# A quantiser's search whose squares are summed 64 wide on VectorE, with GpSimd making chunk products

## The chip, the cores and the metric

The kernel runs on one core of a Trainium2 chip. A core has five engines with a queue of instructions each: TensorE (PE, with its weight loads as PEld) for matrix products, VectorE (DVE), ScalarE (ACT), GpSimd (POOL) and SyncE (SP), which here only starts transfers. The queues run side by side and meet only in semaphores. The metric is the time of one execution on the device, in microseconds, as the median of several.

## The reference

Two transformer-like blocks over x of 4 x 256 x 256. Block 0 is a cross attention and a feed-forward layer whose weights are quantised in the kernel; block 1 is a smooth-quantised gated layer and a layer of product-key experts. The change lies in the quantisation of block 0's feed-forward weights:

```
def mse_quant_dequant(w):                    # w: 1024x256 and 256x1024, in blocks of 64
    wb = w.reshape(O, I // 64, 64)
    amax = jnp.max(jnp.abs(wb), axis=-1, keepdims=True)
    base = jnp.maximum(amax, 1e-08) / QMAX
    ...
    for s in SHRINKS:                        # 16 values, 0.4 to 1.0
        scale = base * jnp.asarray(s, dtype=w.dtype)
        deq = jnp.clip(jnp.round(wb / scale), -QMAX, QMAX) * scale
        err = jnp.sum((deq - wb) ** 2, axis=-1, keepdims=True)
        ...                                  # keep the scale with the least error
    deq = jnp.clip(jnp.round(wb / best_scale), -QMAX, QMAX) * best_scale
...
x = x + _L0_xattn_ref(_layernorm(x, axis=-1), ctx_1024, ...)
x = x + _L0_ffn_ref(_layernorm(x, axis=-1), L0_ffn_w_fc, L0_ffn_w_proj)   # relu(x w_fc^T)^2 w_proj^T
x = x + _L1_xattn_ref(_layernorm(x, axis=-1), fside_BxS2xS2_0, ctx_1024)
x = x + _L1_ffn_ref(_layernorm(x, axis=-1), L1_ffn_Wq, L1_ffn_keys, L1_ffn_e_down, L1_ffn_e_up)
```

## The kernel before

Every engine's program is written out by hand as one queue, and all data sit in one large SBUF tile, `arena`, cut into named pieces. The search for the best scale is the first long stage. The two weight matrices lie as 128 partitions x 4096 columns, four **chunks** of 1024 columns with 16 blocks of 64 in each. A **unit** g (0 to 63) is one chunk with one of the 16 shrink factors.

For each chunk c, VectorE takes the block maxima (`prepare`, L1308 to L1312) and scales the weights (`scale_weights`, L1317); ScalarE takes absolute values (`absolute`, L994) and an upper part (`upper`, L999); GpSimd subtracts to get the lower part (`split`, L332). For each unit:

- ScalarE (odd units, L1005) or VectorE (even units, L1347) clips and rounds the scaled weights into one of eight FP8 buffers (`clip_round`). From unit 8 on it waits until TensorE is done with unit g-6.
- TensorE adds to a pair of PSUM banks (two pairs, by turns) the difference of rounded and exact weights: L553 for a chunk's first two units, later L548, which takes the last but one unit's integers away again, then L560, which adds the new ones.
- ScalarE squares the pair (L1020, L1023) into one of **three** square buffers `qd`.
- GpSimd **folds**: it adds columns 32 to 63 of each block to columns 0 to 31 (L343), into one of four buffers `qf`.
- VectorE sums the 32 columns of each block (`sum_error`, L1352).

After a chunk VectorE chooses the scale (`choose`, L1323 to L1329) and quantises and dequantises the chunk in place (L1334, L1335, L1340). Then TensorE transposes it (`w_transposed`; L431 for chunks 0 and 1, L519 for 2 and 3) and ScalarE copies it out (`weights_out`). Attention, layer norms, the transposes of `e_down` and FFN-1 (`ffn1`, L531, 16 blocks, each followed by a relu, L989, on ScalarE and a square on GpSimd, `square_hidden`, L326) are woven in at fixed units by conditions on g in each engine's loop. FFN-2 (`ffn2`, L592), GUW transposes and everything later come after. The loads of WQ1 and EU are issued when all 64 sums are made.

## Time and profile before

| what | us |
|---|---|
| median of three runs (415.94 to 416.29) | 416.27 |
| the profiled execution | 414.8 |
| its span, first to last instruction | 413.0 |
| PE busy in the span | 346.8 |
| DVE busy | 341.7 |
| ACT busy | 248.3 |
| POOL busy | 170.5 |

Busy times are of the span, and engines run side by side, so they don't add up. Matrix products are pipelined and their ends are modelled. An operation's duration overlaps a little with its neighbour's on the same engine, so sums of durations by group are slightly more than busy time by window.

### The profile page before, as it was taken

Reading aid. Unit: us, or ns where it says so; the run is one execution under the profiler, and the core shown is the slowest. Engines: PE = TensorE matmul, PEld = TensorE weight load, DVE = VectorE, ACT = ScalarE, POOL = GpSimd, SP = SyncE. Lnnn points to the kernel's source line nnn. Section 1 sums busy time; section 2 is a strip of 40 time slices with the busy share of each in tenths; the row PEclk is TensorE's granted clock in tenths of the full one; section 3 lists DMA queues with packets and bytes.
Section 4 is the critical chain, followed back from the end, with each engine's and each line's share of the span. In section 5 each row is a group of like instructions: output and inputs, shape, how many; then the busy total and the mean of one; then the engine's idle time right before and its main releaser. Section 6 shows DMA issues by size and latency. Waiting matters only on the chain.

```text
span 413.0 us, 8385 instructions
## 1 busy us (share of the span) xinstructions
PE 346.8 (84%) x3222; PEld 253.1 (61%) x3222; DVE 341.7 (83%) x877; ACT 248.3 (60%) x371; POOL 170.5 (41%) x203
## 2 busy tenths in 40 slices
PE   2876697738857867979997888999999999989996
PEld 1442474413322323656796776887888888778885
DVE  4999879993898597645878899999989999999950
ACT  4799969967778798312645778864676565211000
POOL 3364654456886989812200110526214127621000
PEclk9999999987997999989999999999899999999999
DMA  8920000000000000350000000000000000000000
GB/s 257 362 79 2 2 0 0 2 1 0 2 0 1 0 2 0 97 160 1 2 0 2 1 2 0 3 2 2 2 5 12 14 2 17 2 14 2 17 14 27
DMA packets 11144, 11.42 MB, mean 28 GB/s; under 512 B 608, under 2 KB 10592, under 8 KB 11104
## 3 DMA queue, kind: packets, MB, share of 16 engines
q1 hardware_dynamic: 11104, 10.88, 8.3%
q8 instruction: 26, 0.43, 0.4%
q14 instruction: 14, 0.11, 0.1%
HBM read 9.83 MB, written 1.05 MB: 26 GB/s over the span
## 4 chain that ended last, share of the span: by engine, by line
DVE 43%; PE 26%; POOL 12%; issue 11%; ACT 6%; DMA 1%; POOLq 0%; DVEq 0%; ACTq 0%
POOL arena L343 10%; PE pair L754 9%; PE pair L592 4%; PE pair L718 3%; DVE i L1554 3%; DVE arena L1614 2%; DVE stats L1274 2%; DVE arena L1352 2%; DVE arena L1610 2%; PE pair L740 2%; DVE s L1548 2%; POOL arena L326 2%; DVE XN L1287 2%; PE pair L531 2%; DVE arena L1317 1%
## 5 line engine op out<-in xcount | busy, mean ns | idle before, releaser
L343 POOL TENSOR_TENSOR arena<-arena 128x512 f32<-128x512 f32 x64 | 89.0, 1403 | 59.0 <-ACT arena L1023 23.3
L718 PE MATMUL pair<-arena,EDT 128*128 128x256 f32 x256 | 60.2, 383 | 0.0
L754 PE MATMUL pair<-EU,arena 128*128 128x256 f32 x256 | 58.4, 382 | 0.6 <-DVE arena L1638 0.6
L1352 DVE TENSOR_REDUCE arena<-arena 128x16 f32<-128x512 f32 x64 | 42.8, 680 | 18.4 <-POOL arena L343 18.3
L548 PE MATMUL pair<-arena,WQ 128*128 128x512 fp8e4 x112 | 35.1, 397 | 22.1 <-ACT arena L1020 18.9
L754 PEld LDWEIGHTS pair<-EU,arena 128*128 128x128 f32 x256 | 47.9, 190 | 7.4 <-issue 1.0
L718 PEld LDWEIGHTS pair<-arena,EDT 128*128 128x128 f32 x256 | 47.1, 190 | 6.5 <-ACT arena L1153 0.2
L393 POOL TENSOR_TENSOR arena<-arena 128x512 f32<-128x512 f32 x20 | 27.1, 1370 | 49.4 <-ACT arena L1145 49.4
L1023 ACT ACTIVATE arena<-pair 128x1024 f32<-128x1024 f32 x32 | 33.3, 1041 | 14.7 <-PE pair L560 14.7
L560 PE MATMUL pair<-arena 128*128 128x512 fp8e4 x128 | 40.5, 399 | 0.0
L1020 ACT ACTIVATE arena<-pair,sq_bias 128x1024 f32<-128x1024 f32 x32 | 36.2, 1131 | 4.6 <-PE pair L560 3.7
L1005 ACT ACTIVATE arena<-arena,clip_bias 128x1024 fp8e4<-128x1024 f32 x32 | 37.2, 1166 | 0.0
L531 PE MATMUL pair<-arena 128*128 128x512 f32 x64 | 34.7, 678 | 1.7 <-ACT arena L980 1.7
L548 PEld LDWEIGHTS pair<-arena,WQ 128*128 128x128 bf16 x112 | 9.9, 101 | 42.4 <-issue 38.8
L1347 DVE TENSOR_SCALAR arena<-arena 128x1024 fp8e4<-128x1024 f32 x32 | 29.7, 930 | 7.0 <-PE pair L560 5.6
L1153 ACT ACTIVATE arena<-pair 128x512 f32<-128x512 f32 x32 | 19.0, 598 | 26.8 <-PE pair L718 26.7
L326 POOL TENSOR_TENSOR arena<-arena 128x512 f32<-128x512 f32 x16 | 20.1, 1260 | 26.0 <-ACT arena L989 26.0
L592 PEld LDWEIGHTS pair<-arena 128*128 128x128 f32 x256 | 29.7, 193 | 1.5 <-issue 1.5
L592 PE MATMUL pair<-arena 128*128 128x128 f32 x256 | 30.2, 276 | 0.0
L1145 ACT COPY arena<-pair 128x512 f32<-128x512 f32 x20 | 19.5, 1070 | 11.1 <-PE pair L740 11.1
L740 PEld LDWEIGHTS pair<-arena 64*128 64x128 bf16 x1536 | 20.1, 93 | 6.2 <-issue 3.2
L370 POOL CAST i12f<-i 128x64 bf16<-128x64 uint32 x8 | 8.0, 1004 | 36.6 <-DVE i L1554 28.9
(196 smaller groups left out, 667.5 us busy)
## 6 DMA issues: line engine op xcount, KB each, us to landing
arena<-in_L_ffn_e_down_dram SPq DMA_DIRECT2D x1, 2048.0 KB, 12.2
EU<-in_L_ffn_e_up_dram SPq DMA_DIRECT2D x1, 2048.0 KB, 9.2
arena<-in_L_ffn_w_fc_dram SPq DMA_DIRECT2D x2, 512.0 KB, 5.3
X<-in_x_dram SPq DMA_DIRECT2D x1, 1024.0 KB, 5.9
arena<-in_L_ffn_w_proj_dram SPq DMA_DIRECT2D x1, 1024.0 KB, 14.6
GUW<-in_fside_BxS2xS_dram SPq DMA_DIRECT2D x1, 1024.0 KB, 12.1
out_dram<-arena SPq DMA_DIRECT2D x8, 128.0 KB, 1.7
CTX<-in_ctx_dram SPq DMA_DIRECT2D x1, 512.0 KB, 4.9
```

The source lines that it names most:

```text
L343: pool.tensor_tensor(qf(g), sq[:, :, 0:32], sq[:, :, 32:64], ALU.add).then_inc(s["folded"], 1)
L531: last = pe.matmul(bank[2 + i % 2], W1T[:, k, m * P:m * P + P], xnT[:, k, half * 512:half * 512 + 512], start=(k == 0), stop=(k == 1))
L548: pe.matmul(to[half], stepN[:, j - 2, :], qr[:, (g - 2) % QDEEP, cols[half]], start=False, stop=False, skip_group_check=True)
L560: last = pe.matmul(to[half], stepI[:, j, :], qr[:, g % QDEEP, cols[half]], start=False, stop=True, skip_group_check=kept)
L592: last = pe.matmul(bk2(F2_BANK[b])[:, n, o * P:o * P + P], h2T[:, k, at:at + P], W2T[:, k, o * P:o * P + P], start=(k == 0), stop=(k == HI ...
L718: last = pe.matmul(bk2(4 + i % 2)[:, r, :], EDT[:, k, at:at + P], xT4[:, b % 2, k, :], start=(k == 0), stop=(k == 1))
L754: last = pe.matmul(bk2(7)[:, n, :], PR[:, n, e, :], EU[:, e, :], start=(e == 0), stop=(e == EROWS - 1))
L1005: act.activation(qr[:, g % QDEEP, :], qu[:, g // NS % 2, :], ACT.Relu, bias=clip_bias[:, 0:1], scale=-GRID / STEPS[g % NS], saturate=False ...
L1020: act.activation(qd[g % 3], pair[2 + g % 2][:, :], ACT.Square, bias=sq_bias[:, g % NS:g % NS + 1]).then_inc(s["squared"], 1)
L1023: act.activation(qd[g % 3], pair[2 + g % 2][:, :], ACT.Square).then_inc(s["squared"], 1)
L1347: dve.tensor_scalar(qr[:, g % QDEEP, :], qu[:, g // NS % 2, :], TB_MAX * STEPS[g % NS], GRID / STEPS[g % NS], ALU.min, ALU.mult, saturate= ...
L1352: dve.tensor_reduce(err[:, g // NS % 2, :, g % NS], qf(g), AX.X, ALU.add).then_inc(s["reduced"], 1)
```

## The change

Nothing is folded any more (`halved` is false for every unit). VectorE's `sum_error` reduces the squares themselves, 128 x 1024, 64 columns a block. There are five square buffers (`QDEPTH`), the two new ones in two places by turns of time. GpSimd takes over, for chunks 1 to 3, `scale_weights`, and for chunks 0 to 2 the product ahead of the rounding (`scale_quantised`) and `dequantise`; it keeps `split` and `square_hidden`. VectorE makes the first `split`. The step tables are made in eight portions with a semaphore each. The loops over g are replaced by lists of calls on each engine, in another order. The arithmetic of each result is otherwise the same.

```diff
+    QDEPTH = 5
-        qd = (cut(22 * KI, CH), cut(23 * KI, CH), cut(7 * KI, CH))
+        qd_early, qd_late = ((cut(22 * KI, CH), cut(23 * KI, CH), cut(7 * KI, CH), cut(a * KI, CH), cut((a + 1) * KI, CH))
+                             for a in (14, 24))
...
+        def halved(g):
+
+            return g < 0
...
+        def qd(g):
+            return (qd_early if g <= QF_LATE else qd_late)[g % QDEPTH]
...
# GpSimd
-            for g in range(NU):
+            def fold(g):
...
-                if g % NS == 12 and g // NS + 1 < NCH:
-                    split(g // NS + 1)
-                if g - 2 in FFN1_UNIT:
-                    square_hidden(FFN1_UNIT[g - 2])
+            def scale_weights(c):
+
+                pool.wait_ge(s["prepared"], c + 1)
+                if c >= 2:
+                    pool.wait_ge(s["diff"], NS * (c - 1))
+                pool.tensor_tensor(blocks(qu[:, c % 2, :]), blocks(W[:, c * CH:c * CH + CH]), spread(rbase), ALU.mult
+                                   ).then_inc(s["scaled"], 1)
+
+            def scale_quantised(c):
+
+                pool.wait_ge(s["chosen"], c + 1)
+                pool.tensor_tensor(blocks(qt), blocks(W[:, c * CH:c * CH + CH]), spread(rscale), ALU.mult
+                                   ).then_inc(s["qscaled"], 1)
+
+            def dequantise(c):
+
+                pool.wait_ge(s["qrounded"], c + 1)
+                pool.tensor_tensor(blocks(W[:, c * CH:c * CH + CH]), blocks(qi), spread(scale), ALU.mult
+                                   ).then_inc(s["wquant"], 1)
...
# ScalarE
+            def square(g):
+
+                act.wait_ge(s["diff"], g + 1)
+                if g >= QDEPTH:
+                    if halved(g - QDEPTH):
+                        act.wait_ge(s["folded"], folds(g - QDEPTH))
+                    else:
+                        act.wait_ge(s["reduced"], g - QDEPTH + 1)
...
# VectorE
             def sum_error(g):
-                dve.wait_ge(s["folded"], g + 1)
-                dve.tensor_reduce(err[:, g // NS % 2, :, g % NS], qf(g), AX.X, ALU.add
-                                  ).then_inc(s["reduced"], 1)
+                if halved(g):
+                    dve.wait_ge(s["folded"], folds(g))
+                    squares = qf(g)
+                else:
+                    dve.wait_ge(s["squared"], g + 1)
+                    squares = blocks(qd(g))
+                dve.tensor_reduce(err[:, g // NS % 2, :, g % NS], squares, AX.X, ALU.add).then_inc(s["reduced"], 1)
...
+            sum_error(47)
+            clip_round(56)
+            sum_error(48)
...
+            sum_error(59)
+            round_quantised(2)
+            sum_error(60)
+            sum_error(61)
+            sum_error(62)
+            sum_error(63)
+            choose(3)
+            scale_quantised(3)
+            round_quantised(3)
+            dequantise(3)
```

Three places show how the order moves. First GpSimd, from the end of its constants to FFN-1's last squares; before:

```order
L343 TENSOR_TENSOR arena<-arena 128x512 x13
L332 TENSOR_TENSOR QP<-arena,QP 128x1024
L343 TENSOR_TENSOR arena<-arena 128x512 x16
L332 TENSOR_TENSOR QP<-arena,QP 128x1024
L343 TENSOR_TENSOR arena<-arena 128x512 x3
L326 TENSOR_TENSOR arena<-arena 128x512
L343 TENSOR_TENSOR arena<-arena 128x512 x4
L326 TENSOR_TENSOR arena<-arena 128x512
```

And after the change, where L372 scales weights, L353 splits, L378 scales for the rounding, L384 dequantises and L347 squares hidden blocks:

```order
L372 TENSOR_TENSOR arena<-arena 128x1024
L353 TENSOR_TENSOR QP<-arena,QP 128x1024
L378 TENSOR_TENSOR arena<-arena 128x1024
L372 TENSOR_TENSOR arena<-arena 128x1024
L353 TENSOR_TENSOR QP<-arena,QP 128x1024
L384 TENSOR_TENSOR arena<-arena 128x1024
L347 TENSOR_TENSOR arena<-arena 128x512 x2
L378 TENSOR_TENSOR arena<-arena 128x1024
L347 TENSOR_TENSOR arena<-arena 128x512
L372 TENSOR_TENSOR arena<-arena 128x1024
L384 TENSOR_TENSOR arena<-arena 128x1024
L353 TENSOR_TENSOR QP<-arena,QP 128x1024
```

The folds are gone, and products of 1024 columns stand between splits and squares. Second VectorE, near the sums of units 16 and 17, where chunk 0's scale is chosen; before (L1352 sums, L1347 clips, L1285 and L1287 a norm):

```order
L1328 TENSOR_TENSOR arena<-arena 128x16
L1329 RECIPROCAL arena<-arena 128x16
L1347 TENSOR_SCALAR arena<-arena 128x1024
L1352 TENSOR_REDUCE arena<-arena 128x16
L1334 TENSOR_TENSOR arena<-arena 128x1024
L1335 TENSOR_SCALAR arena<-arena 128x1024
L1352 TENSOR_REDUCE arena<-arena 128x16
L1285 RECIPROCAL rstd<-rstd 128x2
L1287 TENSOR_SCALAR XN<-X,mv,rstd 128x256 x2
```

And after (L1627 sums, L1617 clips, L1564 to L1570 chunk 2's block maxima, L1603 the rounding):

```order
L1589 TENSOR_TENSOR arena<-arena 128x16
L1590 RECIPROCAL arena<-arena 128x16
L1627 TENSOR_REDUCE arena<-arena 128x16
L1564 TENSOR_REDUCE arena<-arena 128x16
L1565 TENSOR_SCALAR arena<-arena 128x16
L1569 RECIPROCAL arena<-arena 128x16
L1570 TENSOR_SCALAR arena<-arena 128x16
L1617 TENSOR_SCALAR arena<-arena 128x1024
L1627 TENSOR_REDUCE arena<-arena 128x16 x2
L1617 TENSOR_SCALAR arena<-arena 128x1024
```

The product L1334 has left VectorE's queue, and the rounding stands 15 rows behind the reciprocal instead of 4. Third TensorE at the end of the search; before (L519 transposes chunk 3, chunk 2's having stood after unit 58; L592 is FFN-2, x16 one half of a batch):

```order
L548 MATMUL pair<-arena,WQ 128x512 x2
L560 MATMUL pair<-arena 128x512 x2
L531 MATMUL pair<-arena 128x512 x6
L431 MATMUL pair<-ident,GUW 128x128 x4
L592 MATMUL pair<-arena 128x128 x16
L519 MATMUL pair<-ident,arena 128x128 x8
L531 MATMUL pair<-arena 128x512 x2
L592 MATMUL pair<-arena 128x128 x16
```

And after (L608 and L620 are the last unit, L578 transposes, first of chunk 2 and then of chunk 3, L590 is FFN-1, L736 FFN-2):

```order
L608 MATMUL pair<-arena,WQ 128x512 x2
L620 MATMUL pair<-arena 128x512 x2
L578 MATMUL pair<-ident,arena 128x128 x8
L590 MATMUL pair<-arena 128x512 x6
L490 MATMUL pair<-ident,GUW 128x128 x4
L736 MATMUL pair<-arena 128x128 x16
L578 MATMUL pair<-ident,arena 128x128 x8
L590 MATMUL pair<-arena 128x512 x2
```

Chunk 2's transposes now stand between the last unit and the three FFN-1 blocks.

## Rows read from the trace of the kernel before

**Rows 1.** The page: the chain that ended last, share of the span by line.

```profile
POOL arena L343 10%; PE pair L754 9%; PE pair L592 4%; PE pair L718 3%; DVE i L1554 3%; DVE arena L1614 2%; DVE stats L1274 2%; DVE arena L1352 2%; DVE arena L1610 2%; PE pair L740 2%; DVE s L1548 2%; POOL arena L326 2%; DVE XN L1287 2%; PE pair L531 2%; DVE arena L1317 1%
```

**Rows 2.** Windows: length; busy us of PE, PEld, DVE, ACT, POOL; clock, DMA.

```profile
13.10:64.40 51.30, 41.17 (x177) 24.75 (x177) 46.03 (x109) 43.41 (x63) 26.88 (x19) 0.97 0.21 71
64.40:106.40 42.00, 29.23 (x132) 14.81 (x131) 32.99 (x52) 34.51 (x46) 24.84 (x19) 0.92 0.00 1
106.40:171.30 64.90, 49.02 (x172) 20.30 (x171) 52.18 (x67) 51.67 (x58) 56.03 (x40) 0.95 0.00 1
13.10:171.30 158.20, 119.42 (x478) 59.85 (x478) 131.20 (x225) 129.59 (x165) 107.75 (x76) 0.95 0.07 23
...
178.30:413.00 234.70, 218.96 (x2696) 186.14 (x2696) 196.62 (x621) 111.19 (x196) 56.91 (x75) 0.99 0.03 9
```

**Rows 3.** Waits, 13 to 171.3 us: who waited for whom, us, times, longest.

```profile
POOL arena L343 <- ACT arena L1023: 23.3, 11, 10.7
POOL arena L343 <- ACT arena L1020: 22.4, 14, 3.7
...
DVE arena L1352 <- POOL arena L343: 18.3, 19, 1.7
...
POOL arena L343 <- DVE arena L1352: 11.1, 7, 2.0
...
DVE arena L1347 <- PE pair L560: 5.6, 2, 3.9
```

**Rows 4.** Groups on DVE, 0 to 178 us: busy us, mean ns, idle before.

```profile
L1352 DVE TENSOR_REDUCE arena<-arena 128x16 f32<-128x512 f32 x64 | 42.8, 680 | 18.4 <-POOL arena L343 18.3
L1347 DVE TENSOR_SCALAR arena<-arena 128x1024 fp8e4<-128x1024 f32 x32 | 29.7, 930 | 7.0 <-PE pair L560 5.6 <-ACT arena L994 1.2
L1287 DVE TENSOR_SCALAR XN<-X,mv,rstd 128x256 f32<-128x256 f32 x16 | 9.4, 641 | 0.2
L1317 DVE TENSOR_TENSOR arena<-arena 128x1024 f32<-128x1024 f32 x4 | 7.8, 1960 | 0.0
L1334 DVE TENSOR_TENSOR arena<-arena 128x1024 f32<-128x1024 f32 x4 | 6.2, 1547 | 0.0
...
L1340 DVE TENSOR_TENSOR arena<-arena 128x1024 f32<-128x1024 fp8e4 x4 | 5.3, 1336 | 0.0
L1308 DVE TENSOR_REDUCE arena<-arena 128x16 f32<-128x1024 f32 x4 | 4.8, 1209 | 4.3 <-DMA arena<-in_L_ffn_w_fc_dram 4.3
```

**Rows 5.** Groups on POOL, 0 to 178 us.

```profile
L343 POOL TENSOR_TENSOR arena<-arena 128x512 f32<-128x512 f32 x64 | 89.0, 1403 | 59.0 <-ACT arena L1023 23.3 <-ACT arena L1020 22.4 <-DVE arena L1352 11.1
...
L332 POOL TENSOR_TENSOR QP<-arena,QP 128x1024 fp32r<-128x1024 f32 x3 | 7.0, 2349 | 0.0
```

**Rows 6.** Lines by themselves: ns shortest/median/longest, first and last start.

```profile
L1352 DVE TENSOR_REDUCE arena<-arena x64: 655/676/689, 20.0 to 170.6; 128x16 f32<-128x512 f32 x64
...
L1347 DVE TENSOR_SCALAR arena<-arena x32: 662/693/2224, 8.7 to 158.9; 128x1024 fp8e4<-128x1024 f32 x32
...
L1287 DVE TENSOR_SCALAR XN<-X,mv,rstd x32: 400/409/1459, 20.8 to 337.7; 128x256 f32<-128x256 f32 x32
...
L1324 DVE TENSOR_TENSOR arena<-arena x4: 425/746/1460, 64.8 to 171.7; 128x256 f32<-128x256 f32 x4
...
L326 POOL TENSOR_TENSOR arena<-arena x16: 1030/1038/2025, 103.1 to 203.9; 128x512 f32<-128x512 f32 x16
```

**Rows 7.** Timeline: start us, length us, engine, what.

```profile
16.52 1.88 PE L458 MATMUL pair<-ctxT,arena 128*128 128x512 f32 x4
```

**Rows 8.** Timeline at the end of the search.

```profile
166.08 5.31 PE L531 MATMUL pair<-arena 128*128 128x512 f32 x12
...
171.66 3.74 PE L592 MATMUL pair<-arena 128*128 128x128 f32 x32
...
174.97 1.22 DVE L1334 TENSOR_TENSOR arena<-arena 128x1024 f32<-128x1024 f32 x1
...
178.23 1.09 PE L519 MATMUL pair<-ident,arena 128*128 128x128 f32 x8 [2.83 <-DVE arena L1340]
```

More of the change, by code:

```diff
@@ L257, in on_act, with act_rounds @@
         def on_act(g):
-            return 0 < g < NU and g % 2 == 1
+            return g % 2 == 1
+        def act_rounds(g):
+            return sum(on_act(i) for i in range(g + 1))
         @block.sync
@@ L349, in _ @@
+            dequantise(2)
+            square_hidden(7)
             square_hidden(8)
@@ new lines, in _ @@
+            unit(7)
+            probs_transposed(0)
+            x_transposed(1)
+            unit(8)
+            unit(9)
+            x_transposed(2)
+            probs_transposed(1)
+            unit(10)
+            attend(0)
+            probs_transposed(2)
+            unit(11)
+            attend(1)
+            attend(2)
+            unit(12)
+            x_transposed(3)
+            unit(13)
+            unit(14)
+            probs_transposed(3)
+            unit(15)
+            unit(16)
@@ new lines, in _ @@
+            unit(25)
+            unit(26)
+            unit(27)
+            unit(28)
+            x1_transposed(1)
+            unit(29)
+            unit(30)
+            unit(31)
+            unit(32)
+            x1_transposed(2)
+            unit(33)
+            unit(34)
+            w_transposed(0)
+            unit(35)
+            unit(36)
+            x1_transposed(3)
+            unit(37)
+            ffn1(0)
+            unit(38)
+            ffn1(1)
+            ffn1(2)
+            unit(39)
@@ new lines, in _ @@
+            unit(40)
+            ffn1(3)
+            unit(41)
+            unit(42)
+            unit(43)
+            unit(44)
+            unit(45)
+            w_transposed(1)
+            unit(46)
+            unit(47)
+            unit(48)
+            unit(49)
+            unit(50)
+            ffn1(4)
+            unit(51)
+            unit(52)
+            unit(53)
+            unit(54)
+            ffn1(5)
+            unit(55)
+            unit(56)
+            ffn1(6)
+            unit(57)
@@ L587, in ffn2 @@
+            ffn1(7)
+            unit(58)
+            unit(59)
+            unit(60)
+            unit(61)
+            unit(62)
+            unit(63)
+            w_transposed(2)
             def ffn2(b, o, tiles=range(TPB)):
@@ new lines, in _ @@
+            square(8)
+            probs_out(0)
+            absolute(1)
+            probs_out(1)
+            clip_round(11)
+            x_out(2)
+            square(9)
+            square(10)
+            probs_out(2)
+            clip_round(13)
+            clip_round(15)
+            square(11)
+            exponentials(3)
+            square(12)
+            x_out(3)
+            upper(1)
+            square(13)
+            square(14)
+            probs_out(3)
+            square(15)
+            std(0, 2, "ln2")
@@ new lines, in _ @@
+            x1_out(0)
+            clip_round(25)
+            square(23)
+            clip_round(27)
+            e_down_out(5)
+            clip_round(29)
+            square(24)
+            clip_round(31)
+            square(25)
+            absolute(2)
+            upper(2)
+            square(26)
+            square(27)
+            e_down_out(6)
+            square(28)
+            x1_out(1)
+            square(29)
+            square(30)
+            e_down_out(7)
+            square(31)
@@ new lines, in _ @@
+            clip_round(33)
+            square(32)
+            x1_out(2)
+            clip_round(35)
+            square(33)
+            clip_round(37)
+            square(34)
+            square(35)
+            weights_out(0)
+            x1_out(3)
+            square(36)
+            clip_round(39)
+            relu(0)
+            clip_round(41)
+            square(37)
+            relu(1)
+            square(38)
+            relu(2)
+            square(39)
+            clip_round(43)
+            square(40)
@@ new lines, in _ @@
+            clip_round(45)
+            clip_round(47)
+            square(41)
+            square(42)
+            absolute(3)
+            square(43)
+            upper(3)
+            square(44)
+            relu(3)
+            square(45)
+            clip_round(49)
+            square(46)
+            square(47)
+            clip_round(51)
+            square(48)
+            weights_out(1)
+            square(49)
+            clip_round(53)
+            square(50)
+            square(51)
@@ new lines, in _ @@
+            square(52)
+            relu(4)
+            clip_round(55)
+            square(53)
+            square(54)
+            clip_round(57)
+            relu(5)
+            square(55)
+            clip_round(59)
+            square(56)
+            relu(6)
+            square(57)
+            clip_round(61)
+            square(58)
+            clip_round(63)
+            square(59)
+            relu(7)
+            square(60)
+            square(61)
+            square(62)
+            square(63)
@@ L1054, in c_root @@
+            weights_out(2)
             def c_root(b):
```

458 lines of the change are left out of this document (311 added, 147 removed).

## Prediction

> **What bounds the kernel now.** I read the stages first, then the waits, then the groups of instructions, then the chain at the end of the search.
>
> The stages [rows 2] cut the span at 13.1 us (first difference on TensorE done), at 64.4, 106.4 and 171.3 us (last sum of chunks 0 and 1, and of the whole search) and at 178.3 us (last chunk dequantised). The reader is to see that in the search no engine is full: VectorE is busy 131.2 of 158.2 us, ScalarE 129.6, and TensorE 119.4 by modelled ends. After 178.3 us it is another kernel, TensorE busy 219.0 of 234.7 us. So the search counts until 171.3 us, then the seven microseconds in which VectorE makes the last weights, and then TensorE. The chain that ended last [rows 1] names the culprit: the GpSimd fold, L343, first of all lines with a tenth of the span.
>
> The waits of the search [rows 3] show a ring. GpSimd waits 23.3 and 22.4 us for the squares, VectorE 18.3 us for the folds, and GpSimd 11.1 us for sums that free a folded buffer. Every unit passes TensorE, ScalarE, GpSimd and VectorE, with three square buffers between the second and third; VectorE's 27.0 us of idle time (158.2 - 131.2) is the length of this ring, not work. A change that only moved work between engines would gain little; one that shortens the ring can gain up to these 27 us, less what it adds to VectorE.
>
> **The change, part by part.**
>
> *The fold goes, the sum doubles.* A fold took 1.403 us on GpSimd, 64 times [rows 5]; it and its handover leave the ring. A sum over 128x512 took 0.680 us; over 128x1024 there is a row of the same operation and shape of input, L1308, the block maximum, 1.209 us [rows 4]. Difference 0.529 us, times 64: **+33.9 us** on VectorE. The short sums did not stretch beside a busy GpSimd (655 to 689 ns, [rows 6]), so I take this as it is; with those two for the short sum the bounds are +33 and +35.5.
>
> *Chunk products move to GpSimd.* VectorE loses the scaling of chunks 1 to 3 (four took 7.8 us, the first, the fastest, 1.2 of it: 6.6), the first product of the quantiser for chunks 0 to 2 (6.2 less the last, 1.2 [rows 8]: 5.0) and the dequantisation of chunks 0 to 2 (5.3 - 1.2: 4.1) [rows 4]: **-15.7 us**. On GpSimd these nine have no row. From below a fold's 1.4 us for half the elements; from above twice that, 2.8. The nearest row is the 1024-wide subtraction L332, 2.349 us [rows 5], and I take it. Nine are 21 us on an engine that loses 89 us.
>
> *VectorE's short operations stretch less.* Clips on VectorE (L1347) ran between 662 and 2224 ns [rows 6], mean 930 [rows 4]; 32 at 0.66 would be 21.1 us instead of 29.7, so 8.6 us is stretch. The norms (L1287, 16 at 641 [rows 4] against a fastest of 400 [rows 6]) add 3.9, and the 256-wide operations of the choice and of the attention's normalising, which stretch like L1324 (425 to 1460 ns, [rows 6]), about 3.5 by my estimate: 16 us of stretch in all. I put it down to GpSimd running beside them, since the sums, next to the same GpSimd, don't stretch. GpSimd was busy 107.8 us in the search [rows 2]. In the new search it has 12 operations of 2.35 us and eight squares of hidden blocks at about 1.04 (L326, [rows 6]): 36.5 us, a third. So up to two thirds of the stretch, 10.6 us, go. I take **-10 us**; bounds 0 and -12.
>
> The Trainium skill (SBUF — State Buffer, Who interferes with whom) says that VectorE's `tensor_scalar` in its two-port mode, and its operations with two SBUF inputs, contend with GpSimd for one port pair held for a whole instruction, and that `tensor_reduce` on this chip never does. By that rule all of the stretch is GpSimd's, the relief the whole 10.6 us and the time 406.6 us; if the stretch had another cause, the relief would be 0 and the time 417.2. This trace agrees on the reductions (655 to 689 ns).
>
> VectorE's work from 13.1 us to its last sum is then 131.2 + 33.9 - 15.7 - 10 = 139.4 us: with no idle time the last sum would end at 152.5 us instead of 171.3. ScalarE's list is the same instructions in another order, 129.6 us [rows 2]: second, at 142.7 us.
>
> *Idle time that stays.* Five square buffers instead of three, and the order has VectorE summing two to five units behind ScalarE, so a sum seldom waits. But both engines now have over 85% of the stage to do, in fixed queues, each releasing the other, and in the first 16 units attention is woven in: there VectorE already was busy 46.0 of 51.3 us [rows 2] and now gets 16 longer sums (+8.5 us) and loses one product (2.0) and some stretch. This part gains next to nothing; the gain must come after 64.4 us, where VectorE was busy 33.0 of 42.0 and 52.2 of 64.9 us. I estimate 8 us of idle (between 3 and 16), some 5% of the stage. So the last sum ends near 13.1 + 139.4 + 8 = 160.5 us: **-10.8 us**.
>
> *The start.* TensorE now does the first attention input, 1.9 us at 16.5 us before [rows 7], ahead of unit 0, and VectorE makes step tables in eight portions. I cost this at nothing: up to 20 us VectorE has statistics, tables, clips and the second block maximum to do. Without that cover it costs the 1.9 us.
>
> *The end.* Before, the last unit was followed on TensorE by three FFN-1 blocks (from 166.08 us, 5.3 us), the first gate-weight transpose and half an FFN-2 group (3.74 us from 171.66 us), finished by 175.4 us; it then waited 2.83 us for the last dequantised chunk and began its transposes at 178.23 us [rows 8]. Now the transposes of chunk 2 stand in front of this run, after unit 63, and they need that chunk dequantised by GpSimd. VectorE rounds it four sums, 4.8 us, ahead of the end; with 2.35 us of GpSimd, 1.1 of transposes (as L519, [rows 8]) and the rest of the copies on ScalarE, 0.6 by my estimate, the three FFN-1 blocks start about 0.7 us before the last sum ends instead of 5.2 us before. Their run of 9.4 us (166.08 to 175.4) ends 8.7 us after it, where the last chunk's transposes could begin 7.0 us after it (178.23 - 171.25). **+1.7 us**, bounds 0 and +4. From there TensorE is nearly full and the order is kept, so later stages shift as a block. The two loads that wait for the last sum (WQ1 and EU) also move as a block.
>
> Sum: -10.8 + 1.7 = -9.1 us. The profiled execution took 414.8 us (span 413.0); the median of the three runs shown is 1.5 us more. 414.8 - 9.1 = 405.7, so a median of **407.2 us**.
>
> **Rivals.**
>
> *A, the queues fit almost without gaps.* For it: five buffers, and clips and sums interleaved unit by unit. Against it: ScalarE alone would keep the search going to 142.7 us. Idle time 3 instead of 8 us: 402.2 us.
>
> *B, the two full engines stop each other more.* Idle 13 instead of 8 us, mostly in the attention units: 412.2 us. For it: VectorE was idle only 5.3 us there before, with lighter sums, and now each stall pushes back sums that hold square buffers.
>
> *C, slower: clips wait at the head of VectorE's queue.* The clip of unit g waits for TensorE to be done with unit g-6, and sums stand behind it (clip 56 stands behind sum 47 and needs unit 50). Before, this happened twice, 5.6 us together [rows 3], 2.8 each. Each such wait stops the engine that is now the bound. One is within my 8 us. The gain is gone when more than three others appear (9.1 / 2.8); with four the time is 418.4 us. Against it: VectorE runs behind TensorE when it is the bound, and then the unit is long done.
>
> *D, slower: GpSimd's longer instructions hold VectorE.* A clip that took 2.22 us instead of 0.66 shows a block of about one fold. If half of each of GpSimd's 36.5 us blocked a VectorE operation, stretch would be 18 us, more than now, where the forecast keeps 6: 419.2 us. It turns slower from 15 us of stretch on. Read strictly, the Trainium skill (SBUF — State Buffer, Who interferes with whom) would have it so, as the later engine there waits for the whole instruction; against that, in this trace 107.8 us of GpSimd came with 16 us of stretch, a seventh.
>
> **How the numbers follow.** My forecast 62%, A 12%, B 11%, C 9%, D 6%. A, the forecast and nearly all of B are faster by over 0.2% (0.8 us, about what a measurement of this kernel can tell); B's end and the light ends of C and D give 5% for within 0.2%, and their rest 11% for slower. The range reaches from the middle of A to past B: 402 to 415 us; it leaves out the fast half of A and most of C and D, and holds the bounds of stretch (-12 gives 405.2; 0 gives 417.2, outside, and counts with D) and of the end (405.5 to 409.5).
>
> **What the new profile would show.** 64 sums near 1.2 us each; the VectorE clips' mean down from 930 ns to below 800; VectorE busy 93% or more from 13 us to the last sum, that sum ending near 160.5 us; chunk 0's sums done at 63 to 66 us as before; GpSimd products near 2.35 us and its share of the span from 41% to about 25%; TensorE starting the last chunk's transposes about 9 us after the last sum. I am wrong if long sums take more than 1.25 us, if clips wait for TensorE more than twice, or if VectorE is idle over 16 us in the search.

## The result, and the profile after

The changed kernel takes 389.81 us (median of 4 runs, 389.28 to 390.5), the kernel before, timed beside it, 416.11 us (4 runs, 414.91 to 416.29): a ratio of 0.9375, 95% interval 0.9351 to 0.9398. The gain is 26 us where 9 were forecast: 389.8 us lies below the range of 402 to 415.

First the windows of the changed kernel, to be laid beside [rows 2]: from the first difference to the last sum of the search, the part before chunk 0's choice (it begins at 64.4 us in both kernels), from the last sum to the last chunk's first transpose, and from there to the end.

```profile
13.10:147.20 134.10, 111.76 (x465) 55.55 (x464) 131.84 (x224) 127.81 (x163) 33.53 (x20) 0.96 0.08 28
13.10:64.40 51.30, 46.28 (x221) 27.91 (x220) 49.87 (x120) 50.03 (x74) 4.37 (x2) 1.00 0.21 71
147.20:155.80 8.60, 8.60 (x48) 5.92 (x47) 8.29 (x10) 1.79 (x3) 3.38 (x3) 1.00 0.91 292
155.80:387.90 232.10, 217.29 (x2698) 185.66 (x2696) 195.40 (x621) 111.09 (x196) 59.29 (x75) 0.99 0.02 7
```

The last sum ends at 147.2 us instead of 171.3. VectorE's busy time in the search is what it was, 131.8 us, but the window is 24 us shorter: its idle time went from 27.0 to 2.3 us. ScalarE, 127.8 us busy, is now close behind it. The last chunk's transposes start 8.6 us after the last sum (before 7.0), and everything behind them takes 232.1 us instead of 234.8.

The chain that ended last, by engine and by line, no longer has GpSimd in it (the fold led it in [rows 1]):

```profile
DVE 53%; PE 25%; ACT 10%; issue 8%; DMA 2%; SPq 1%; POOL 0%; DVEq 0%; ACTq 0%
DVE arena L1627 10%; PE pair L898 7%; PE pair L736 5%; DVE i L1966 4%; DVE arena L1617 3%; DVE s L1960 3%; DVE arena L2026 3%; PE pair L590 3%; DVE arena L2022 2%; ACT arena L1167 2%; ACT arena L1164 2%; DVE XN L1552 2%; PE pair L884 2%; DMA arena<-in_L_ffn_keys_dram 2%; DVE pk L1981 2%
```

The groups of VectorE in the search, 13.1 to 147.2 us (busy us, mean ns, idle before), with their lines answering to [rows 4]:

```profile
L1627 DVE TENSOR_REDUCE arena<-arena 128x16 f32<-128x1024 f32 x64 | 75.8, 1207 | 0.0
L1617 DVE TENSOR_SCALAR arena<-arena 128x1024 fp8e4<-128x1024 f32 x29 | 20.2, 697 | 0.0
L1640 DVE TENSOR_SCALAR arena<-ident 128x128 bf16<-128x128 f32 x14 | 4.7, 334 | 0.0
L1552 DVE TENSOR_SCALAR XN<-X,mv,rstd 128x256 f32<-128x256 f32 x8 | 2.9, 409 | 0.1
L1659 DVE TENSOR_SCALAR XN<-X,mv,rstd 128x256 f32<-128x256 f32 x8 | 2.9, 405 | 0.0
```

The sums have the forecast length and never wait. The clips (L1617, before L1347) fell from a mean of 930 ns [rows 4] to 697, the norms from 641 to about 407. GpSimd's products, up to 156 us, are a little shorter than forecast:

```profile
L353 POOL TENSOR_TENSOR QP<-arena,QP 128x1024 fp32r<-128x1024 f32 x3 | 7.1, 2359 | 33.3 <-ACT QP L1143 33.3
L372 POOL TENSOR_TENSOR arena<-arena 128x1024 f32<-128x1024 f32 x3 | 6.6, 2188 | 15.3 <-DVE arena L1570 15.2
L384 POOL TENSOR_TENSOR arena<-arena 128x1024 f32<-128x1024 fp8e4 x3 | 6.1, 2027 | 8.6 <-DVE arena L1603 8.6
L378 POOL TENSOR_TENSOR arena<-arena 128x1024 f32<-128x1024 f32 x3 | 5.7, 1901 | 16.5 <-DVE arena L1590 16.5
```

### The profile page after: what moved, and what is told of

The parts are those of the page before. It is cut to its first block, busy times and chain, and to the rows that moved or that the text cites. A ratio compares the mean times of both kernels' runs of the same rounds, so it can differ in the third digit from the quotient of the medians.

```text
span 387.9 us, 8250 instructions
## 1 busy us (share of the span) xinstructions
PE 342.5 (88%) x3222; PEld 250.7 (65%) x3222; DVE 343.1 (88%) x868; ACT 247.7 (64%) x371; POOL 99.6 (26%) x148
## 4 chain that ended last, share of the span: by engine, by line
DVE 53%; PE 25%; ACT 10%; issue 8%; DMA 2%; SPq 1%; POOL 0%; DVEq 0%; ACTq 0%
DVE arena L1627 10%; PE pair L898 7%; PE pair L736 5%; DVE i L1966 4%; DVE arena L1617 3%; DVE s L1960 3%; DVE arena L2026 3%; PE pair L590 3%; DVE arena L2022 2%; ACT arena L1167 2%; ACT arena L1164 2%; DVE XN L1552 2%; PE pair L884 2%; DMA arena<-in_L_ffn_keys_dram 2%; DVE pk L1981 2%
## 5 line engine op out<-in xcount | busy, mean ns | idle before, releaser
L1627 DVE TENSOR_REDUCE arena<-arena 128x16 f32<-128x1024 f32 x64 | 75.8, 1207 | 0.0
L608 PE MATMUL pair<-arena,WQ 128*128 128x512 fp8e4 x112 | 35.8, 403 | 13.8 <-ACT arena L1164 8.8
L620 PE MATMUL pair<-arena 128*128 128x512 fp8e4 x128 | 40.5, 399 | 2.9 <-DVE arena L1617 2.9
L452 POOL TENSOR_TENSOR arena<-arena 128x512 f32<-128x512 f32 x20 | 27.4, 1383 | 45.0 <-ACT arena L1410 45.0
L347 POOL TENSOR_TENSOR arena<-arena 128x512 f32<-128x512 f32 x16 | 16.9, 1055 | 60.4 <-ACT arena L1133 60.4
L736 PEld LDWEIGHTS pair<-arena 128*128 128x128 f32 x256 | 30.7, 199 | 1.0 <-issue 1.0
L736 PE MATMUL pair<-arena 128*128 128x128 f32 x256 | 31.2, 282 | 0.0
L608 PEld LDWEIGHTS pair<-arena,WQ 128*128 128x128 bf16 x112 | 8.7, 101 | 34.3 <-ACT arena L1164 13.3
L590 PE MATMUL pair<-arena 128*128 128x512 f32 x64 | 29.7, 597 | 0.9 <-ACT arena L1126 0.7
L1410 ACT COPY arena<-pair 128x512 f32<-128x512 f32 x20 | 19.6, 1071 | 9.9 <-PE pair L884 9.9
L620 PEld LDWEIGHTS pair<-arena 128*128 128x128 bf16 x128 | 12.3, 102 | 20.2 <-issue 4.7
L884 PE MATMUL pair<-arena 64*128 64x32 bf16 x1536 | 21.7, 173 | 2.2 <-DVE arena L2044 1.3
L1617 DVE TENSOR_SCALAR arena<-arena 128x1024 fp8e4<-128x1024 f32 x32 | 22.2, 697 | 1.1 <-ACT arena L1138 1.1
## 6 DMA issues: line engine op xcount, KB each, us to landing
arena<-in_L_ffn_e_down_dram SPq DMA_DIRECT2D x1, 2048.0 KB, 12.2
GUW<-in_fside_BxS2xS_dram SPq DMA_DIRECT2D x1, 1024.0 KB, 12.4
```

The source lines that it names most:

```text
L590: last = pe.matmul(bank[2 + i % 2], W1T[:, k, m * P:m * P + P], xnT[:, k, half * 512:half * 512 + 512], start=(k == 0), stop=(k == 1))
L608: pe.matmul(to[half], stepN[:, j - 2, :], qr[:, (g - 2) % QDEEP, cols[half]], start=False, stop=False, skip_group_check=True)
L620: last = pe.matmul(to[half], stepI[:, j, :], qr[:, g % QDEEP, cols[half]], start=False, stop=True, skip_group_check=kept)
L736: last = pe.matmul(bk2(F2_BANK[b])[:, n, o * P:o * P + P], h2T[:, k, at:at + P], W2T[:, k, o * P:o * P + P], start=(k == 0), stop=(k == HI ...
L884: last = pe.matmul(bank[scatter_bank(t, half) + r][:, g16 * JW:g16 * JW + JW], oh[rows, g // NG, :, g % NG], wc[rows, c, g // NG, :, g % N ...
L1617: dve.tensor_scalar(qr[:, g % QDEEP, :], qu[:, g // NS % 2, :], TB_MAX * STEPS[g % NS], GRID / STEPS[g % NS], ALU.min, ALU.mult, saturate= ...
```

## The experiments

Twelve kernels, in three groups of four (e1 to e4, e5 to e8, e9 to e12). Each group was timed beside its own runs of the kernel before, with medians of 414.75, 414.61 and 414.89 us, against 416.11 beside the changed kernel; single runs of that one kernel reach from 411.6 to 417.0 us. So a difference of medians across groups is good to 1 or 2 us. Below, "window" is the time from 13.1 us to the last sum and "idle" is the window less VectorE's busy time in it, from one profile each; ratios are to the kernel before.

| kernel | median us | ratio, 95% | window | DVE busy | idle | POOL busy |
|---|---|---|---|---|---|---|
| before | 416.11 | 1 | 158.2 | 131.2 | 27.0 | 107.7 |
| e1_direct | 417.27 | 1.003 [0.9995, 1.007] | 160.3 | 140.9 | 19.4 | 15.8 |
| e2_direct_five | 407.16 | 0.979 [0.972, 0.987] | 152.6 | 141.9 | 10.7 | 15.7 |
| e3_five | 416.09 | 1.000 [0.996, 1.004] | 160.2 | 129.7 | 30.5 | 109.2 |
| e4_three | 402.27 | 0.970 [0.963, 0.976] | 145.6 | 133.2 | 12.4 | 34.6 |
| e5_products | 397.43 | 0.957 [0.951, 0.963] | 141.7 | 138.3 | 3.5 | 16.2 |
| e6_load | 410.02 | 0.986 [0.980, 0.992] | 153.3 | 151.5 | 1.8 | 93.5 |
| e7_fold_all | 411.08 | 0.991 [0.988, 0.995] | 153.3 | 125.7 | 27.6 | 123.9 |
| e8_w2late | 414.23 | 0.999 [0.995, 1.002] | 157.9 | 132.0 | 25.9 | 106.5 |
| e9_load_short | 398.58 | 0.965 [0.958, 0.972] | 140.5 | 139.0 | 1.5 | 90.3 |
| e10_lag4 | 411.26 | 0.991 [0.986, 0.995] | 154.0 | 141.8 | 12.2 | 16.0 |
| e11_fold6 | 391.31 | 0.945 [0.938, 0.951] | 135.1 | 132.7 | 2.4 | 41.9 |
| e12_fold12 | 389.67 | 0.943 [0.937, 0.950] | 133.2 | 129.9 | 3.3 | 49.8 |
| after | 389.81 | 0.9375 [0.935, 0.940] | 134.1 | 131.8 | 2.3 | 33.5 |

### Direct sums alone (e1_direct)

The kernel before, without folds:

```diff
-                pool.tensor_tensor(qf(g), sq[:, :, 0:32], sq[:, :, 32:64], ALU.add).then_inc(s["folded"], 1)
...
-                    act.wait_ge(s["folded"], g - 2)
+                    act.wait_ge(s["reduced"], g - 2)
...
-                dve.tensor_reduce(err[:, g // NS % 2, :, g % NS], qf(g), AX.X, ALU.add
+                dve.tensor_reduce(err[:, g // NS % 2, :, g % NS], blocks(qd[g % 3]), AX.X, ALU.add
```

> The kernel before with one part of the change: no fold, VectorE sums 64 columns straight from the squares; order, three square buffers and VectorE's chunk products stay. VectorE's work would be 131.2 + 33.0 - about 12 of stretch that leaves with the folds, some 152 us. Theory 'handover' (the idle 27 us were the fold's place in the ring): idle falls to about 6 us, last sum near 171 us, 412 to 418 us in all, so no clear gain from this part alone. Rival 'order' (the new order fills the gaps): idle stays near 20 us, 425 us or more. If it comes out under 405 us, stretch from GpSimd was worth far more than I think.

No gain: 417.3 us, inside the 412 to 418 that I expected, but by luck, since two errors cancelled. Idle time stayed at 19.4 us, the rival's figure, where I had expected about 6; and VectorE's work came to 140.9 us, not 152. The sums cost what they should, yet VectorE's busy time rose by only 9.7 us, so some 24 us of it went: the stretch. Groups of VectorE in its search, which answer to [rows 4]:

```profile
L1340 DVE TENSOR_SCALAR arena<-arena 128x1024 fp8e4<-128x1024 f32 x31 | 21.2, 687 | 9.5 <-PE pair L553 5.2 <-ACT arena L987 4.1
L1280 DVE TENSOR_SCALAR XN<-X,mv,rstd 128x256 f32<-128x256 f32 x16 | 5.6, 407 | 0.2
L1310 DVE TENSOR_TENSOR arena<-arena 128x1024 f32<-128x1024 f32 x3 | 3.6, 1216 | 0.0
L1302 DVE TENSOR_SCALAR arena<-arena 128x16 f32<-128x16 f32 x3 | 0.8, 272 | 0.1
L1321 DVE TENSOR_TENSOR arena<-arena 128x16 f32<-128x16 f32 x3 | 0.5, 175 | 0.1
```

L1310 is the scaling that took 1960 ns before (a mean of four, [rows 4]). The last two are operations of 16 columns, which in the kernel before were:

```profile
L1309 DVE TENSOR_SCALAR arena<-arena 128x16 f32<-128x16 f32 x3 | 2.3, 777 | 0.1
L1328 DVE TENSOR_TENSOR arena<-arena 128x16 f32<-128x16 f32 x3 | 1.6, 526 | 0.1
```

Summed over all groups of the same form, leaving out sums and products, VectorE's stretch in the kernel before was 20 us, and 4 us more sat in its products. The rest of the window is waits: with three square buffers and direct sums, ScalarE waits 12 us for VectorE's sums, and VectorE is idle for 19.4 us.

### Five buffers, with and without the folds (e2_direct_five, e3_five)

```diff
-        qd = (cut(22 * KI, CH), cut(23 * KI, CH), cut(7 * KI, CH))
+        qd_early, qd_late = ((cut(22 * KI, CH), cut(23 * KI, CH), cut(7 * KI, CH), cut(a * KI, CH), cut((a + 1) * KI, CH))
+                             for a in (14, 24))
...
-                if g >= 3:
-                    act.wait_ge(s["folded"], g - 2)
+                if g >= 5:
+                    act.wait_ge(s["reduced"], g - 4)
```

(e3 keeps the folds and waits on "folded" there.)

> As e1, with five square buffers instead of three, in the order of before. Theory 'handover': with only two steps behind TensorE the buffers hardly matter, within 2 us of e1. Rival 'buffers': five buffers take up the jitter of the two full engines, 5 us or more under e1.

> The kernel before with five square buffers and nothing else (folds stay). Rival 'buffers': GpSimd may fall behind without stopping ScalarE, 408 us or less. Theory 'handover': ScalarE waited for GpSimd only 0.9 us before, so 414 to 416 us.

In e2 my theory fell and the rival held: with direct sums the two added buffers cut the idle time from 19.4 to 10.7 us and are worth 10 us. With the folds they are worth nothing, 416.1 us: VectorE still waits 19.7 us for GpSimd's folds (18.3 before, [rows 3]). In the order of before, the buffers help only once the fold is off the ring.

### The new order with three buffers (e4_three), and with VectorE's own products (e5_products)

e4 is the changed kernel with one number:

```diff
-    QDEPTH = 5
+    QDEPTH = 3
```

> The changed kernel with three square buffers instead of five. Theory 'handover with the new order': VectorE is planned two to five units behind, which three buffers don't allow; ScalarE waits for sums, and with both engines over 90% busy that costs 5 to 10 us: 395 to 400 us. Rival: buffers don't matter, 390 to 391 us.

By the medians it gives 12.5 us back, more than the 5 to 10 that I expected, and 10.1 of them are idle time. Waits of VectorE in its search:

```profile
DVE arena L1617 <- PE pair L620: 5.4, 3, 4.2
DVE rsum L1671 <- ACT arena L1096: 2.0, 1, 2.0
DVE arena L1627 <- ACT arena L1167: 2.0, 2, 1.4
```

The first is the wait of the prediction's rival C, a clip at the head of the queue that TensorE has not freed. With three buffers it is there; with five it is gone.

e5 is the changed kernel with its nine products on VectorE, at the places that they had relative to the sums:

```diff
-            scale_weights(1)
...
-            dequantise(2)
...
+            scale_weights(1)
...
+            dequantise(2)
```

> The changed kernel with the nine chunk products back on VectorE (beside the block maxima, and each ahead of and behind its rounding). They would take about 1.22 us each beside a quiet GpSimd, 11 us, or 15.7 us if they stretch as before. VectorE is the bound with 2 us of idle time, so all of it shows: 400 us (399 to 403). Rival: the stretch that remains comes from GpSimd's products, and leaves with them, 397 us or less.

7.6 us slower than the changed kernel, 397.4 us: between my 399 to 403 and the rival's 397, since part of the rival's effect is there. The products take 11.6 us there (1.2 to 1.4 us each); VectorE's other operations lose 5 us of length for GpSimd's 17.4 us less. Against e2, which has the same instructions in the old order, e5 is 9.7 us faster, 7.2 of it idle time: that is what the order brings, to within 1 or 2 us.

### A busy GpSimd without a fold to wait for (e6_load, e9_load_short)

The changed kernel, with additions on GpSimd that nobody reads: 44 of 128x512 (e6, whose edit is shown), or 110 of 128x128 (e9). GpSimd waits for two more semaphores ahead of them, VectorE for none.

```diff
+            def load(n, at):
+                for _ in range(n):
+                    link(pool.tensor_tensor(cut(at * KI, 512).rearrange("p (n c) -> p n c", n=4), CTX[:, 0:4, :],
+                                            CTX[:, 4:8, :], ALU.add))
...
+            load(20, 4)
```

> The changed kernel with 44 more 128x512 additions on GpSimd in the search, about 50 us, into parts of SBUF that nothing uses at the time and in places where GpSimd waited; nothing waits for them. Theory 'stretch' (GpSimd beside VectorE lengthens clips, norms and the choice by about 0.15 us for each us of GpSimd): 7 us more, 396 to 398 us, clips' mean up from 697 to about 850 ns, sums unchanged near 1.207. Rival (the stretch of before had other causes): within 1 us of 390.

> The changed kernel with 110 additions of 128x128 elements on GpSimd during the search, whose results nobody reads, in place of the run before last's 44 of 128x512. Theory (VectorE is stretched by a share of the time that GpSimd works): the added busy time of GpSimd times the 0.33 us per us that the 44 long additions cost; at 0.35 to 0.5 us each they add 38 to 55 us, so 12 to 18 us more than the changed kernel, 402 to 408 us. Rival (a VectorE clip is held until the GpSimd instruction in progress ends, so what counts is the length of one instruction): short additions hold it by 0.2 us at most, VectorE's mean clip stays under 0.75 us, 391 to 396 us.

e6, groups of VectorE up to 166.4 us, and the added work:

```profile
L1640 DVE TENSOR_REDUCE arena<-arena 128x16 f32<-128x1024 f32 x64 | 75.7, 1206 | 0.0
L1630 DVE TENSOR_SCALAR arena<-arena 128x1024 fp8e4<-128x1024 f32 x29 | 24.2, 833 | 0.4 <-PE pair L633 0.4
L1653 DVE TENSOR_SCALAR arena<-ident 128x128 bf16<-128x128 f32 x14 | 9.5, 680 | 0.0
L1565 DVE TENSOR_SCALAR XN<-X,mv,rstd 128x256 f32<-128x256 f32 x8 | 7.0, 910 | 0.1
...
L389 POOL TENSOR_TENSOR arena<-CTX 128x512 f32<-128x512 f32 x44 | 60.0, 1364 | 3.0
```

e9, the same two kinds of line:

```profile
L1639 DVE TENSOR_REDUCE arena<-arena 128x16 f32<-128x1024 f32 x64 | 75.7, 1205 | 0.0
L1671 DVE TENSOR_SCALAR XN<-X,mv,rstd 128x256 f32<-128x256 f32 x8 | 4.4, 589 | 0.0
...
L389 POOL TENSOR_TENSOR arena<-CTX 128x128 f32<-128x128 f32 x110 | 56.6, 515 | 8.1
```

VectorE's idle time stays below 2 us, yet e6 is 20 us slower: 60 us of GpSimd cost VectorE 19.6 us, 0.33 us per us. I had expected 0.15, and was wrong. The sums did not move from 1.21 us. In e9 nearly as much GpSimd time (56.6 us) in pieces of 0.5 us cost 7.2 us, 0.13 per us. What a piece can hold shows in the longest clip, here the line of the clips in e6 and in e9 (shortest, median, longest):

```profile
L1630 DVE TENSOR_SCALAR arena<-arena x32: 675/684/1750, 8.6 to 158.4; 128x1024 fp8e4<-128x1024 f32 x32
```

```profile
L1629 DVE TENSOR_SCALAR arena<-arena x32: 675/693/959, 8.7 to 145.6; 128x1024 fp8e4<-128x1024 f32 x32
```

The longest clip is 1.07 us over the median in e6 and 0.27 us in e9. The timeline of the one in e6 shows what it met (start, length):

```profile
40.87 1.26 POOL L389 TENSOR_TENSOR arena<-CTX 128x512 f32<-128x512 f32 x1
40.93 1.75 DVE L1630 TENSOR_SCALAR arena<-arena 128x1024 fp8e4<-128x1024 f32 x1
```

The clip starts 0.06 us into an addition and ends 0.55 us after it, where a clip by itself takes 0.68. In e9 the longest clip starts beside an addition of 0.46 us, at 93.43 us, and ends 0.55 us after it too. The other held operations follow the same pattern. None of the reductions was held, but 28 of VectorE's other operations in e6's search are more than 0.1 us over the shortest of their form in any of these traces, and 44 in e9's. Each of them started while a GpSimd instruction ran, and is over by what that instruction still had to go, less 0.09 to 0.25 us. So the hold goes by the GpSimd instruction in progress. The longest holds of all, 2.05 us in e6 and 1.75 in e9, came beside the changed kernel's own `split` and product. GpSimd is held as well: an addition of 128x512 has a median of 1.27 us and a longest of 1.66, one of 128x128 a median of 0.46 and a longest of 0.92, so its busy time holds some of its own waiting. The time of e9 fell between its two expectations, though: its clips' mean was 797 ns, not under 750, since 110 short holds add up too.

By the Trainium skill (SBUF — State Buffer, Who interferes with whom), a VectorE instruction that needs the port pair shared with GpSimd and a GpSimd instruction lock each other out for a whole instruction, and a reduction on this chip never contends. These runs agree on both: 64 sums at 1206 ns beside a GpSimd that is 61% busy, and holds that shrink with the length of the instruction.

### All folds back, and some (e7_fold_all, e11_fold6, e12_fold12)

The changed kernel's own switch, with each fold placed in GpSimd's program:

```diff
         def halved(g):
-            return g < 0
+            return g in (7, 14, 22, 33, 47, 58)
```

(This is e11. e7: every unit. e12: twelve. In all three a few chunk products also change places with squares in GpSimd's program.)

> The changed kernel's order, five buffers and GpSimd products, but with every unit folded on GpSimd again and short sums on VectorE. VectorE's work falls by 33 us and rises by some 12 us of stretch to about 113 us; ScalarE has 128 us and GpSimd 33.5 + 85. Theory 'order': the new order alone carries the gain, ScalarE becomes the bound, 385 to 392 us. Theory 'handover': fold and its handover stand in every unit again, idle time returns, 400 us or more.

> The changed kernel with 6 of 64 units folded by GpSimd, as its switch allows. Each fold takes 0.53 us of summing off VectorE and puts 1.3 to 1.4 us on GpSimd, which at 0.33 us of stretch per us gives 0.45 us back. Theory: within 1 us of 389.8 us. Rival (a sum that waits for its fold leaves VectorE idle, as in the kernel with every unit folded): about 0.4 us each, 392 us.

> The changed kernel with 12 of 64 units folded. Theory as for 6 folds: 12 x (0.53 - 0.45), 1 us, within 1.5 us of 389.8 us. Rival (waits for folds): 394 us or more.

e7 has the new order and five buffers, and takes 411.1 us, all but 3.5 us of the old time. Its groups of VectorE:

```profile
L1691 DVE TENSOR_REDUCE arena<-arena 128x16 f32<-128x512 f32 x64 | 42.8, 675 | 26.1 <-POOL arena L365 26.1
L1681 DVE TENSOR_SCALAR arena<-arena 128x1024 fp8e4<-128x1024 f32 x29 | 29.7, 1024 | 0.0
L1737 DVE TENSOR_SCALAR arena<-arena,rsum 128x256 f32<-128x256 f32 x8 | 8.6, 1109 | 0.1
```

Both costs of a fold are in it. Sums wait 26.1 us for folds, more than the 18.3 of before; and though the sums are 33 us shorter than in the changed kernel, VectorE's busy time is only 6.1 us less: 90 us of GpSimd gave the rest back. With 12 folds the price of stretch and the saving cancel, as expected: 389.7 us against 389.8. With 6 it is 391.3 us, between my theory (within 1 us) and the rival (392). The intervals of both overlap with the changed kernel's, so neither gain nor loss is shown. The waits for folds are 1.1 us in e12.

### Sums one unit later (e10_lag4)

e2 with each sum issued four units behind its scores:

```diff
-                if g >= 3:
-                    sum_error(g - 3)
+                if g >= 4:
+                    sum_error(g - 4)
```

> The kernel before with no folds, direct sums of 64 and five buffers, its own order, but each sum issued four units behind its scores in place of three. Theory (what the new order takes out of VectorE's idle time is the wait of sums for squares that ScalarE has not written yet): the idle time before the last sum falls from 10.7 to about 6 us, 403 to 404 us. Rival (ScalarE then waits for a buffer that VectorE frees later, and the gain goes back; the order of the other steps is what counts): within 1 us of 407.2 us.

My theory fell: 411.3 us, idle 12.2 instead of 10.7. Waits of VectorE in its search:

```profile
DVE arena L1346 <- PE pair L557: 5.0, 2, 4.7
DVE X L1395 <- PE pair L481: 3.5, 2, 3.3
DVE arena L1351 <- ACT arena L1019: 0.6, 1, 0.6
```

The sums' waits for squares did shrink (2.9 us in e2, 1.1 here), but the clip's wait for TensorE doubled (2.5 us in e2). The rival's reason, a buffer freed later, isn't in the trace: ScalarE waits 0.7 us for a sum here. The clip's 4.7 us, from 95.0 to 99.7 us, show something else in the window over them, and so does TensorE's timeline:

```profile
95.02:99.70 4.68, 4.68 (x9) 1.58 (x8) 0.04 (x1) 1.15 (x3) 0.00 (x0) 0.50 0.00 0
```

```profile
94.06 3.78 PE L528 MATMUL pair<-arena 128*128 128x512 f32 x4 [1.71 <-ACT arena L977]
```

TensorE was busy throughout, at a granted clock of 0.50, and its FFN-1 block took 3.78 us, where the same four matmuls take 1.88 at a clock of 1.00. The longest clip waits of before (3.9 us) and of e2 (1.9 us) stand behind the same block, also at half clock. So part of VectorE's idle time in the old order comes from TensorE's clock. Of the 4.1 us between e2 and e10 only 1.4 lie before the last sum; the rest is later. So what the new order removes is not one wait. In e2 VectorE has seven idle gaps above 0.5 us, the longest 2.2: a residual behind attention, clips behind TensorE, sums behind ScalarE. Which of the order's moves removes which was not tried.

### The last transposes without a pause (e8_w2late)

The kernel before, with chunk 2's transposes after the last unit, as in the changed kernel:

```diff
-        W_UNIT = {27: 0, 42: 1, 58: 2}
+        W_UNIT = {27: 0, 42: 1, 63: 2}
```

> The kernel before with chunk 2's transposes behind the last unit instead of unit 58, as in the changed kernel. TensorE then has no 2.8 us gap ahead of the last chunk's transposes. Theory 'clock': these come 1 to 2 us later after the last sum, and the granted clock stays 1.00 behind them where it fell to 0.52 for 3.2 us, which gives back 1.6 us: within 1 us of before. Rival: the clock falls anyway, and the time is 1.5 us or more longer.

Before, TensorE stood idle for 2.83 us ahead of the last transposes [rows 8]. The same stretch of TensorE's timeline right behind them, in the kernel before:

```profile
179.16 3.48 PE L531 MATMUL pair<-arena 128*128 128x512 f32 x4
```

and in e8, where TensorE comes to them without a pause:

```profile
178.81 1.04 PE L519 MATMUL pair<-ident,arena 128*128 128x128 f32 x8
179.69 1.88 PE L531 MATMUL pair<-arena 128*128 128x512 f32 x4
```

The same four matmuls take 3.48 and 1.88 us. Windows over them, of before and of e8:

```profile
179.20:182.40 3.20, 3.20 (x6) 1.18 (x5) 0.80 (x2) 0.80 (x2) 0.00 (x0) 0.52 0.35 110
```

```profile
179.80:182.40 2.60, 2.60 (x14) 1.64 (x13) 0.35 (x1) 1.32 (x3) 0.12 (x1) 1.00 0.10 29
```

The granted clock is 0.52 against 1.00, its lower level (1.2 GHz) against the higher (2.4 GHz), after 2.83 us of idle time and after none. The half clock cost 1.6 us on these matmuls. That the pause brought it is likely but not shown, as this is one trace against one. In e3 a pause of 1.36 us at the same place was followed by a clock of 1.00. And e8 has a half clock of its own, earlier:

```profile
161.00:167.80 6.80, 5.69 (x15) 2.41 (x16) 3.23 (x5) 4.50 (x5) 6.80 (x6) 0.50 0.00 0
```

It falls while TensorE stands idle for 2.69 us, up to 162.11 us. In total e8 is 0.4 us faster by the medians, within what can be told.

## Why the prediction was wrong

The sign held, and the parts of the change work as described. Four steps failed: the relief of stretch and the idle time were mis-sized, both in the same direction, the overlap of records was left out, and the later stages were put at no change. By the profiled executions 405.7 us was forecast and 389.7 came, 16.0 us less (by the medians 17.4, as the profiled execution of before lay further under its median than that of the changed kernel):

| step | forecast | measured | difference |
|---|---|---|---|
| VectorE's work to its last sum | 139.4 | 131.8 | -7.6 |
| idle time that stays | 8 | 2.3 | -5.7 |
| last transposes after the last sum | +1.7 | +1.6 | -0.1 |
| later stages | 0 | -2.7 | -2.7 |

**Sums: right.** 64 at 1.207 us; the difference, without overlap, is 33.0 us (forecast 33.9). **Products: right.** The nine took 15.7 us of VectorE before, and GpSimd's take 1.9 to 2.4 us.

**"VectorE's short operations stretch less": too small, and with it the bound of -12.** Over the groups of the same form, leaving sums and products out, 14.3 us of stretch went, not 10. The share was right: GpSimd's busy time fell by 69%, the stretch by 72%. The size to which I applied it was too small: e1, with GpSimd 16 us busy, shows 20 us of stretch in the kernel before, where I had added up 16 from clips, norms and a few 256-wide operations. What I had left out were operations of 16 columns, 777 ns before and 272 in e1, 3.1 us in all, and the roundings of chosen chunks (L1335), 1.4 us.

**Missing: the overlap of records.** I added differences of mean durations to a busy time, which is a union. Where the next instruction waits for nothing it starts 0.08 us before the end of the one before, as the changed kernel's timeline shows (start, length):

```profile
86.62 0.68 DVE L1617 TENSOR_SCALAR arena<-arena 128x1024 fp8e4<-128x1024 f32 x1
87.22 1.21 DVE L1627 TENSOR_REDUCE arena<-arena 128x16 f32<-128x1024 f32 x1
88.35 0.68 DVE L1617 TENSOR_SCALAR arena<-arena 128x1024 fp8e4<-128x1024 f32 x1
```

The sum of 1.21 us occupies 1.13. Busy time by group, in which overlap inside a group is already taken out, adds up to 138.5 us before (busy 131.2) and 142.9 after (busy 131.8): the overlap grew from 7.3 to 11.1 us, 3.8 us that my sum did not have. Against that stand 1.4 us of work that I costed at nothing: step tables now made inside the window, 4.7 us, less 3.3 us of clips, statistics and a maximum that left it. In all: -4.3 (stretch) -0.9 (sums) -3.8 (overlap) +1.4 gives the -7.6 us.

**"Idle time that stays: 8 us": 2.3.** Rival A was nearly right here (3 us), and so was its reason, that the queues fit. The prediction took the 27.0 us of before for the length of the ring through the fold. That was only part of it: 19.4 us stayed when the fold alone left the ring (e1), and 10.7 with five buffers as well (e2). e4 shows the other side. With three buffers the same order leaves 12.4 us, with five 2.3. Without the order five buffers leave 10.7 (e2). That the attention units gain next to nothing was right: chunk 0's choice begins at 64.4 us as before, with 18 sums done instead of 17. The choices of chunks 1, 2 and 3 then begin at 97.2, 130.6 and 147.2 us, where they began at 106.0, 143.9 and 171.3. What failed is the estimate for that later part, in which I let two nearly full engines stop each other.

**"Later stages shift as a block": they gained 2.7 us.** The two traces can be laid side by side, one TensorE instruction against the same one in the other kernel. At the last transposes the kernel before is 22.4 us behind. Behind the half clock that follows its pause it is 24.0, so 1.6 us of the gain are made there. The next 1.7 us come at 292 to 295 us, where its granted clock was 0.51 and that of the changed kernel, at the same work, 1.00. Over the rest 0.7 us are lost again, to 25.1. The changed kernel has a half clock too:

```profile
200.20:203.60 3.40, 3.31 (x16) 3.12 (x17) 3.26 (x11) 1.11 (x3) 0.00 (x0) 0.50 0.00 0
```

It cost nothing: before, TensorE waited 1.44 us for VectorE behind this work, and now it doesn't. Other traces have such half clocks elsewhere (e3 at 256 and 372 us, e8 at 291), so these 2.7 us belong in part to the two executions profiled and not to the change. No experiment isolates them.

**The rivals.** C did not appear with five buffers and did with three. B and D did not appear: products on GpSimd are worth 7.6 us (e5), because what they hold up of VectorE, 5 us, is less than the 11.6 us that they took there. D's mechanism is real all the same: a long GpSimd instruction does hold VectorE. It lost because the change takes away far more GpSimd time than it adds, and e6 and e7 show how the gain goes when it does not: with GpSimd back at 93 to 124 us, 20 and 21 of the 26 us are gone.

Taken along a path, by the medians: direct sums +2.5 us (e1, against 414.75, with an interval that holds no change), five buffers -10.1 (e2), the order -9.7 (e5), products on GpSimd -7.6 (after). Taking the folds out, or adding buffers, gains nothing alone. With the folds left in, order, buffers and products together gain 3.5 us (e7), and with three buffers the rest of the change gains 12.5 (e4). The order with folds and without GpSimd's products was not tried.

## What to carry to other kernels

Moving work from VectorE to a helping GpSimd has two prices that don't show on the moved line: the handover in the ring, and a hold on VectorE's other two-input and scalar operations, here 0.26 to 0.33 us for each us of GpSimd work in instructions of 1.3 us or more. To size such a hold, compare every group of VectorE with its fastest instance, the smallest operations too, and subtract the overlap of records before adding mean durations. Test parts of a change that share a ring together as well as alone: removing the fold and adding buffers were each worth nothing here, and 7.6 us together.

## What the runs showed of the hardware

- VectorE held up by GpSimd: 0.26 us per us when all folds go (24 us for 92, e1), 0.29 for the products (e5) and for all folds (26 us for 90, e7), 0.33 for independent additions of 1.36 us (e6), 0.13 for additions of 0.5 us (e9). Reductions from 128x1024 stayed at 1.21 us in all of them. Single operations were over by what the running GpSimd instruction still had to go, less 0.09 to 0.25 us (28 operations in e6, 44 in e9).
- On GpSimd an addition of 128x128 took 457 ns (median, e9) and one of 128x512 1271 ns (e6). By the difference that is 2.1 ns a column and 0.19 us for each instruction. The means, 515 and 1364 ns, hold waits for VectorE too.
- After 2.83 us of idle time TensorE's granted clock was 0.52 over the next 3.2 us, and four matmuls took 3.48 us instead of 1.88. After 1.36 us of idle time (e3) it was 1.00. Half clocks also came inside the search, and there a VectorE clip waited 4.7 us for TensorE (e10).
